# Graph network kernel: normalization and table writes between layers moved into neighbouring pipelines, the final scatter into the last hop

## What is computed

```python
edge_index = jnp.stack([src, dst])
h = jnp.maximum(_layernorm(x, axis=-1), 0.0)
x = x + _L0_gnn_ref(edge_index, h)          # 3 hops, grouped by src
h = jnp.maximum(_layernorm(x, axis=-1), 0.0)
x = x + _L1_gnn_ref(h, edge_attr_32, ...)   # MLP messages, sum by dst, layernorm
h = jnp.maximum(_layernorm(x, axis=-1), 0.0)
x = x + _L2_gnn_ref(h, edge_index)          # 3 hops, grouped by dst
h = jnp.maximum(_layernorm(x, axis=-1), 0.0)
x = x + _L3_gnn_ref(edge_index, h)          # 3 hops, grouped by dst
# one hop: x = segment_sum(w[:, None] * x[src], dst); out = out + x; at the end out / 4
```

## Time and profile before

| | us |
|---|---|
| runs (three), lowest / median / highest | 9963.71 / 9969.62 / 10013.37 |
| profiled execution, its own time | 10019.39 |
| its span in the trace | 10017.7 |
| busy: TensorE matmul | 6852.6 (68%) |
| busy: VectorE | 5368.5 (54%) |
| busy: ScalarE | 3631.6 (36%) |
| busy: GpSimd | 6775.8 (68%) |

### The profile page before, as it was taken

One profiled execution on the slowest core, in us unless ns is written; L12 is line 12 of the kernel. 1 busy time (PEld: TensorE's weight loads), 2 busy tenths in 40 slices (PEclk: granted clock), 3 DMA queues, 4 the chain that ended last, 5 costly groups with the idle time before them and its releaser, 6 DMA issues. The chain is left out here.

```text
span 10017.7 us, 117643 instructions
## 1 busy us (share of the span) xinstructions
PE 6852.6 (68%) x25794; PEld 5061.9 (51%) x25794; DVE 5368.5 (54%) x21147; ACT 3631.6 (36%) x11422; POOL 6775.8 (68%) x6677
## 2 busy tenths in 40 slices
PE   7599786708879644448888068787882587989800
PEld 4355443306767533336666056666671466767600
DVE  9799898704422333336666556666667665221210
ACT  0011111104411333335555556666675565111100
POOL 7777777777657777777776066665770575767677
PEclk9899999855555555555555555555555555555555
DMA  6222211246668544433333487888886887985611
GB/s 141 56 58 47 54 21 40 66 55 148 137 82 106 102 100 96 98 83 98 97 95 83 100 112 122 108 119 112 104 107 131 128 125 106 100 91 76 72 41 39
DMA packets 1874472, 916.11 MB, mean 91 GB/s; under 512 B 1662957, under 2 KB 1700905, under 8 KB 1873861
## 3 DMA queue, kind: packets, MB, share of 16 engines
q0 software_dynamic: 213248, 215.45, 26.6%
q1 hardware_dynamic: 795544, 499.16, 18.5%
q10 hardware_dynamic: 865196, 196.73, 9.8%
HBM read 629.66 MB, written 286.87 MB: 91 GB/s over the span
## 5 line engine op out<-in xcount | busy, mean ns | idle before, releaser
L1427 POOL DMA_INDIRECT work<-table,end_idx x3136 | 3136.8, 1000 | 2012.9 <-issue 920.0
L957 PE MATMUL bank<-work 128*128 128x64 f32 x7056 | 2423.8, 448 | 1397.6 <-DMA work<-table,end_idx 1220.9
L960 PE MATMUL bank<-work 32*128 32x64 f32 x7820 | 2679.6, 444 | 342.5 <-ACT work L969 339.3
L957 PEld LDWEIGHTS bank<-work 128*128 128x128 f32 x7056 | 1765.3, 310 | 1821.0 <-issue 1416.7
L960 PEld LDWEIGHTS bank<-work 32*128 32x128 f32 x7820 | 1945.1, 308 | 816.2 <-ACT work L969 377.5
L302 ACT ACTIVATE work<-work 128x64 f32<-128x64 f32 x5488 | 2099.4, 432 | 496.1 <-DVE work L293 434.0
L969 ACT ACTIVATE work<-bank 32x64 f32<-32x64 f32 x3920 | 850.3, 217 | 2563.4 <-PE bank L960 2064.9
L269 DVE BATCH_NORM_STATS2 work<-work 128x6 f32<-128x64 f32 x5488 | 739.2, 211 | 796.1 <-ACT work L302 737.5
L1656 POOL DMA_INDIRECT acc<-nodes,work x784 | 794.5, 1013 | 287.3 <-issue 226.1
L638 POOL DMA_INDIRECT acc<-node_tab,acc x784 | 770.6, 983 | 258.7 <-issue 258.7
L899 DVE TENSOR_TENSOR work<-work,skey_col 128x896 f32<-128x896 f32 x504 | 547.8, 1087 | 241.3 <-DMA work<-skey 119.1
(11 more groups left out here) (165 smaller groups left out, 8203.1 us busy)
## 6 DMA issues: line engine op xcount, KB each, us to landing
work<-skey SPq DMA_DIRECT2D x560, 448.0 KB
table<-work ACTq DMA_DIRECT2D x336, 224.0 KB, 7.1
work<-table,end_idx POOLq DMA_INDIRECT x3136
work<-xd SPq DMA_DIRECT2D x84, 448.0 KB, 4.0
nodes<-zeros ACTq DMA_DIRECT2D x8, 3136.0 KB, 35.8
work<-lowrow SPq DMA_DIRECT2D x196, 128.0 KB, 3.0
work<-in_x SPq DMA_DIRECT2D x56, 448.0 KB, 4.0
nodes<-work ACTq DMA_DIRECT2D x56, 448.0 KB, 3.8
```

Source lines behind the costliest of these rows:

```text
L957: ins = nc.tensor.matmul(o, sel[:, k, :], rows[:, k, :], start=True, stop=not before)
L960: ins = nc.tensor.matmul(o, self.join[b % 2][:, k, :], self.inn[(b + k + 1) % 2], start=False, stop=True)
L1427: nc.gpsimd.indirect_dma_start(got[b][:, k, :], None, source, bass.IndirectOffsetOnAxis(ap=idx[:, t:t + 1], axis=0)).then_inc(got_in[b].se ...
```

## The change

Two of the three `between` stages are gone, and the third is merged into the last hop. Their work goes to the pipelines in front of them.

- mlp_layer makes four buffers of its result rows, normalizes them once more (ln_h, two sets), writes the rows with a quarter of h added to xd and the scaled h to table 0. The slots' drain grows from three to six.
- hop gets `fresh` (the first hop of a layer writes acc in place of adding to it), `next_table` (load xd, add the scaled acc, normalize, store xd and the next layer's table) and `final` (load xd, add, scatter to `out`).
- The hops change places: dense 2 goes to the first hop of layer 3, dense 3 to the second, the third hop of layer 2 carries the update.

The core of the diff:

```diff
 # mlp_layer, ScalarE, slot g (k = 0..6, after first(g))
                             if k == G - 1 and age(i, b, 1):
                                 sums.hand_on(act, i, b - 1, g - 1, G)
+                            if age(i, b, 4):
+                                f = (b - 4) % 4
+                                if k == 0:
+                                    ln_h[b % 2].root(act, i * 4 + (b - 4) // 2)
+                                    if reused(i, b, 8):
+                                        act.wait_ge(s_st[f], i * 64 + (b // 4 * 32 - 32))
+                                ln_h[b % 2].apply(act, o[f], hh[f], ACT.Relu, i * 4 + (b - 4) // 2, range(k, k + 1))
-                        if age(i, b, 3):
-                            act.wait_ge(s_out, g - 2)
-                            act.dma_start(oview[g - 3], o[(b - 3) % 2]).then_inc(s_st[(b - 3) % 2], 16)
+                        if age(i, b, 5):
+                            f = (b - 5) % 4
+                            act.wait_ge(s_y, g - 4)
+                            act.dma_start(oview[g - 5], o[f]).then_inc(s_st[f], 16)
+                            act.dma_start(yview[g - 5], hh[f]).then_inc(s_st[f], 16)
 # mlp_layer, VectorE: end of finish, and a new step
+                        dve.wait_ge(s_out, g + 1)
+                        ln_h[b % 2].stats(Chain(dve, s_dve_h, g * Norm.STEPS), o[b % 4], i * 4 + b // 2)
+                    def leave(i, b, g):
+                        f = b % 4
+                        ln_h[b % 2].done(dve, i * 4 + b // 2)
+                        nc.vector.scalar_tensor_tensor(o[f], hh[f], 0.25, o[f], ALU.mult, ALU.add).then_inc(s_quart, 1)
+                        dve.wait_ge(s_quart, g + 1)
+                        nc.vector.tensor_tensor(hh[f], hh[f], bcast(isq[:, bass.ds(g * G, G)], C), ALU.mult
+                                                ).then_inc(s_y, 1)
 # mlp_layer, VectorE, slot g
                         if age(i, b, 0):
                             ln_in.shift(dve, g)
+                        if age(i, b, 4):
+                            ln_h[b % 2].shift(dve, i * 4 + (b - 4) // 2)
+                        if age(i, b, 5):
+                            leave(i, b - 5, g - 5)
                         if age(i, b, 3):
                             finish(i, b - 3, g - 3)
 # hop, SyncE, last step of load(g)
+                    def load_rows(i, b, g):
+                        f = b % 4
+                        if reused(i, b, 4):
+                            if final:
+                                sp.wait_ge(fin_out[f].sem, uses(i, b, 4) * (16 * G) + fin_out[f].at)
+                            else:
+                                sp.wait_ge(s_ust[f], uses(i, b, 4) * 32)
+                        sp.dma_start(ucur[f], uview[g]).then_inc(s_uin[f], 16)
 # hop, ScalarE, step k of group g
+                            if next_table is not None and reused(i, b, 2):
+                                update_rows(i, b - 2, k)
+                            if next_table is not None and reused(i, b, 3) and k == G - 1:
+                                update_store(b + 1, g - 3)
 # hop, VectorE, post
+                            if fresh:
+                                nc.vector.tensor_scalar(ac, ps, 1.0, None, ALU.mult).then_inc(s_acc, 1)
+                        if update:
+                            dve.wait_ge(s_acc, g * 2 + 2)
+                            nc.vector.scalar_tensor_tensor(acc[:, cols, :], acc[:, cols, :], 0.25,
+                                                           bcast(isq[:, cols], C), ALU.mult, ALU.mult
+                                                           ).then_inc(s_uscale, 1)
+                            dve.wait_ge(s_uin[b % 4], uses(i, b, 4) * 16 + 16)
+                            dve.wait_ge(s_uscale, g + 1)
+                            nc.vector.tensor_tensor(ucur[b % 4], ucur[b % 4], acc[:, cols, :], ALU.add
+                                                    ).then_inc(s_usum, 1)
+                            if not final:
+                                dve.wait_ge(s_usum, g + 1)
+                                uln[b % 2].stats(Chain(dve, s_udve, g * Norm.STEPS), ucur[b % 4], i * 4 + b // 2)
 # hop, GpSimd, final: after the gathers of group g, the scatters of group g-2
+                        if final and g >= 2:
+                            send(g - 2)
 # the list of phases
-        for layer in (2, 3):
-            between(layer == 3, False)
-            hop(1, table[0], end_idx[:, 1, :], to_table=table[1], dense=0 if layer == 2 else 3)
-            hop(1, table[1], end_idx[:, 1, :], to_table=table[0], dense=1 if layer == 2 else None)
-            hop(1, table[0], end_idx[:, 1, :], dense=2 if layer == 2 else None)
-        between(True, True)
+        hop(1, table[0], by_dst, to_table=table[1], fresh=True, dense=0)
+        hop(1, table[1], by_dst, to_table=table[0], dense=1)
+        hop(1, table[0], by_dst, next_table=table[1])
+        hop(1, table[1], by_dst, to_table=table[0], fresh=True, dense=2)
+        hop(1, table[0], by_dst, to_table=table[1], dense=3)
+        hop(1, table[1], by_dst, final=True)
```

More of the change, by code:

```diff
@@ L1228, in _, with hop @@
                     dve.wait_ge(s_acc, 2 * NG)
-        def hop(a, source, idx, to_table=None, to_nodes=None, dense=None, ordered=None, base=False):
+        def hop(a, source, idx, to_table=None, to_nodes=None, dense=None, ordered=None, base=False, fresh=False,
+                next_table=None, final=False):
             ph.next()
@@ L1235, in hop @@
             put_out = [ph.landed(f"put{b}", 16 * G * (NG // 2) if to_nodes is not None else 0) for b in range(2)]
+            update = final or next_table is not None
+            fin_out = [ph.landed(f"fin{b}", 16 * G * (NG // 4) if final else 0) for b in range(4)]
+            s_uin, s_ust = ([ph.sem(f"{n}{f}") for f in range(4)] for n in ("u_in", "u_st"))
+            s_udve, s_usum, s_uout, s_uscale, s_uq = (
+                ph.sem(n) for n in ("u_dve", "u_sum", "u_out", "u_scale", "u_quarter"))
             s_sel, s_tab, s_acc, s_scat, s_bdone, s_bdve = (
@@ L1246, in hop @@
             sums = Sums("h", a, [(2 * b, 2 * b + 1) for b in range(NB)])
+            if update:
+                ucur = [take(G, C) for _ in range(4)]
+                uview = xd.rearrange("(g k p) d -> g p k d", k=G, p=P)
+            if next_table is not None:
+                uh = [take(G, C) for _ in range(4)]
+                uln = [Norm(f"nu{f}", G) for f in range(2)]
+                tview = next_table[0:E, :].rearrange("(g k p) d -> g p k d", k=G, p=P)
             if base:
@@ L1328, in load @@
                             load_base(i, b)
+                        if update:
+                            load_rows(i, b, g)
                         f = b % 2
@@ L1395, in _ @@
                         apply_stage(NT, -1, range(DH))
-                    store(NT, 0, NG)
+                    if to_table is not None:
+                        store(NT, 0, NG)
+                    if next_table is not None:
+                        for n in (NG - 2, NG - 1):
+                            act.wait_ge(s_ust[n % 4], n // 4 * 32)
+                            for k in range(G):
+                                update_rows(0, n, k)
+                        for n in (NG - 3, NG - 2, NG - 1):
+                            update_store(n, n)
+                        for f in range(4):
+                            act.wait_ge(s_ust[f], 32 * (NG // 4))
                     if base:
@@ L1432, in _ @@
                             scatter(g - 2)
+                        if final and g >= 2:
+                            send(g - 2)
+                    if final:
+                        for g in (NG - 2, NG - 1):
+                            send(g)
+                        for p in fin_out:
+                            pool.wait_ge(p.sem, p.end)
                     if to_nodes is not None:
@@ L1471, in post, with update_out @@
                                                     ).then_inc(s_scat, 1)
+                    def update_out(i, b, g):
+                        uln[b % 2].done(dve, i * 4 + b // 2)
+                        nc.vector.scalar_tensor_tensor(ucur[b % 4], uh[b % 4], 0.25, ucur[b % 4], ALU.mult, ALU.add
+                                                       ).then_inc(s_uq, 1)
+                        dve.wait_ge(s_uq, g + 1)
+                        nc.vector.tensor_tensor(uh[b % 4], uh[b % 4], bcast(isq[:, bass.ds(g * G, G)], C), ALU.mult
+                                                ).then_inc(s_uout, 1)
                     def base_stats(i, b, n):
@@ L1535, in turn @@
                             rows_in(i, b)
+                            if next_table is not None and reused(i, b, 2):
+                                uln[b % 2].shift(dve, i * 4 + (b - 2) // 2)
+                            if next_table is not None and reused(i, b, 3):
+                                update_out(i, b - 3, g - 3)
```

(15 more changed lines are left out.)

157 lines of the change are left out of this document (37 added, 120 removed).

## The result

The changed kernel takes 10253.18 us (median of 4, 10233.13 to 10255.92) against 9991.5 us of the kernel before beside it (median of 4, 9963.71 to 10013.98). The ratio is 1.0259 with a 95% interval of 1.0222 to 1.0296: **slower, by 2.6%**. The forecast was 10218 us, with a range of 10110 to 10390. The profiled execution took 10253.8 us, its span is 10252.1 us; that of the kernel before had 10017.7.

The account below looks back on a forecast made before the run. No single engine bounds the whole; the MLP is a program-order chain over three engines. 622 - 503.3 + 48 + 97 - 15 = +248.7 us made the profiled 10019.39 into 10268, less 50 for the median: 10218 us, range 10110 to 10390.

Parts of the forecast that it names:

- the one new wait: MLP slot: VectorE's ln_h.shift waits for ScalarE's root after first(g), with later VectorE work behind it; slot +11.6 us.
- MLP: MLP stage: slots 4 to 55 grow by 11.6 us each, +603 us, and the drain by 19; +622 us.
- Stages between layers: The two whole stages between layers, 248.7 and 254.6 us, are removed: -503.3 us.
- Dense 2's hop: Dense stage 2 moves from a hop without table write (570.5) into one with it (618.5): +48 us.
- First two hops: First two hops of layer 2: same work and tables, a copy of equal size replaces an add; 0.
- Dense 3's hop: The hop with dense 3 keeps its work and its tables: 0.
- Third hop: Layer 2's third hop, with the update: keys queue behind a wait for stores; 636 us against 539.1, +97.
- a recurrence: Third hop: S(g+2) = S(g) + 9.7 + L1 + L2, landings taken as 5.5 and 6.8, so 11.0 us per group.
- Last hop and scatter: Last hop and final stage merge, GpSimd issuing gathers and scatters in turn: 1028 against 1043.1 us, -15.
- Sum: Whole kernel: 622 - 503.3 + 48 + 97 - 15 = +248.7 us, profiled execution becoming 10268 us.
- The median: Whole kernel: runs' median lies 50 us below the profiled execution; same difference applied to 10268, giving 10218 us.
- The first rival: MLP: moved work fills idle time, stage only +70, sum -303, total 9666 us, faster than before; chance 0.07.

Follow-up runs that it names:

- the second pair: The unedited kernel before and changed kernel, profiled again on one chip; changed kernel 10147.45 us, ratio 1.0234.
- the edit of one line: Changed kernel with ScalarE's root of the moved normalization at the start of the MLP slot (early root): 9691.39 us, ratio 0.9666 to the kernel before.
- the root in the middle: Changed kernel with the same moved root put behind ScalarE's two copies out of PSUM: 9990.09 us, ratio 0.9984 to the kernel before.
- the rows behind the keys: Changed kernel with the third hop's row loads issued one group later on SyncE: 10229.45 us, ratio 1.0210 to the kernel before.

## Why the prediction was right, and where its terms were off

The view that decided was the timeline of one MLP slot, and the step was to follow the one new wait through program order. It held in each link: the root at 10.74 us (10.86 forecast), messages ready at 20.37 (20.55), TensorE's start at 20.84 (20.6), the slot 31.01 (30.56), VectorE's idle time 10.56 (10.7), TensorE's 11.19 (about 10), GpSimd's 13.32 (about 12). Three runs back it from three sides: one takes the delay away, one cuts it by 4.59 of its 10.74 us, one takes away what is queued behind it.

The terms, forecast against the first pair of profiles and the second pair:

- **MLP:** +622; +647 and +646. Mis-sized by 25. The slot was 0.45 us longer than the sum, over 52 slots 23 us. The first part is the 0.24 us by which TensorE starts later. The second is the tail, 10.17 in place of 9.96: the row of the last root shows 0.30 us of issue ahead of it. I had put the second store's issue at 0.38 us and wholly beside the last activation; it took 0.53 (5225.01) and stands out behind it.
- **Stages between layers:** -503.3, both gone, right.
- **Dense 2's hop:** +48 against the hop of its kind; +29.6 measured (600.1 - 570.5). With the second stage between layers, -206.6 was forecast for the two; -225.0 and -223.3 measured. The price was taken from the 618.5 of a hop which itself took 602.8 afterwards.
- **First two hops:** 0; -30 and -25 together. The copy costs what the add costs, as assumed; why the hops are shorter is open.
- **Dense 3's hop and what runs ahead of the MLP:** 0; +5 each in the first pair. In the second pair the hop was 15 us shorter, and what runs ahead of the MLP 42 us longer, with the same code.
- **Third hop:** +97; +94 and +81. The size was right by luck, the mechanism in part only. I had used landings of 5.5 and 6.8 us in a recurrence; they were 3.5 to 4.4 for the stores and 5.3 for the keys, which puts two groups at 9.7 + 4.4 + 5.3 = 19.4 us, or 9.7 a group, and 20 us for filling: 563 us in all. The rest of the 633 was not in my sum. And the keys' place behind the wait, which I named as what is new, turned out to be exchangeable: with them ahead of it the hop stayed where it was. The depth of four buffers is worth 25 us, the rows' traffic some 23, and 43 remain that no run takes apart: the added instructions, their order, or longer gathers.
- **Last hop and scatter:** -15; -13 and -19.
- **Sum:** +248.7 forecast; +234.4 between the first two spans. On the profiled execution's own time this was 10268, 14 us too high.
- **The median:** I took the 50 us between the profiled execution and the median as a constant offset. It was none: the kernel before falls into two groups of times (9963.71 and 9969.62; 10013.37, 10013.98 and the profiled 10019.39), and the changed kernel's four lie within 23 us. This one step made 10268 into 10218 and put the forecast 35 us low.

The first rival, that the moved work goes into idle time, was refuted for this change and is true of the kernel that the edit of one line makes of it. Its price of +70 for the MLP measures 97.5 with the root at the start. The Trainium skill's "Perfetto Trace Analysis", section "Optimization Strategy", which says that interleaving regimes may help, is thus borne out here, by a saving of 3.3%, once no instruction that others queue behind waits. The same section says that the same gap, repeating, can mean too few buffers. Both cases are here: the 25 us of the third hop agree with it, while the MLP's gap of 10.6 us in each slot went away with the same buffers and another order.

## What to carry to other kernels

When work is moved into a pipeline to fill idle time, don't ask whether the engine has room; find the new wait, where in the period its releaser stands, and what is queued behind the waiting instruction. In a loop that is one chain over several engines each microsecond by which the awaited instruction comes late, once the slack is used up, is a microsecond of the period (4.59 and 4.54 us here), and the cure is an order: release early, or put the waiting instruction behind what the next engine needs. Where a buffer's way back is store, landing, load, landing, count its length in periods; moving the wait to another place of the same queue only changes who is seen waiting.

## What the runs showed of the hardware that I had not expected

- The same kernel takes 10017, 9932 or 9927 us in the median in the three groups of runs, and what differs is the hops and not the MLP: with the early root the MLP took 1238.3 us in the first group and 1237.2 in the second, the hop behind it 600.2 and 587.4. In the two pairs of profiles the kernel before took 1140.8 and 1141.4 us for the MLP, and 539.1 and 520.4 for the plain hop.
- What runs ahead of the MLP, which no edit touched, ends at 4385 to 4398 us in most profiles and at 4349.6 to 4364.0 in three of them (the kernel before in the last group, the root in the middle, the rows behind the keys). A total from one profiled execution carries these 40 us; a stage's time doesn't.
- The median landing of the table's 224 KB stores in the third hop was 2.9 us without the rows' streams, 4.4 with four row buffers, and 6.6 and 9.3 in two profiles with eight. What else is in flight is not all of it: in the plain hop of the kernel before, with the same code, it was 9.5 us (2.4 to 21.8) in the profile that the prediction read, where the hop took 539.1 us, and 3.6 (2.4 to 7.1) in the later one with 520.4. The far end of 9.5 us in the prediction's sum was thus one execution's.
- The Trainium skill, "DMA: Bandwidth & Descriptors", section "Latency and other measured facts", gives about 2 us of fixed cost; single stores of 224 KB landed after 2.4 us at the least in these two hops, and the fixed part alone was not measured.
